# Self attention on one Trainium2 core: the maximum pass takes three operand pairs of two heads at a time, in two row groups of TensorE, and the two small transposes of a unit move into the middle of a key tile

## What is computed

```python
q = (src @ q_w).reshape(b, s, h, hd).transpose(0, 2, 1, 3)
k = (src @ k_w).reshape(b, s, h, hd).transpose(0, 2, 1, 3)
v = (src @ v_w).reshape(b, s, h, hd).transpose(0, 2, 1, 3)
scores = jnp.einsum('bhqd,bhkd->bhqk', q, k) / np.float32(np.sqrt(hd))
scale = jax.nn.sigmoid(jnp.einsum('bhsd,hd->bhs', q, scale_w)) * 2.0
scores = scores * scale[..., None]
aw = jax.nn.softmax(scores, axis=-1)
out = jnp.einsum('bhqk,bhkd->bhqd', aw, v).transpose(0, 2, 1, 3).reshape(b, s, d)
```

## Time and profile before

| | us |
|---|---|
| median of three runs (2272.37 to 2284.99) | 2282.37 |
| the profiled execution, whole | 2276.61 |
| its span in the trace | 2274.9 |
| self attention, first `first_scores` to the last transpose | 394.6 to 1225.4 |
| one unit in the steady part | 24.69 |

### The profile page before, as it was taken

The page is one execution under the profiler, slowest core; times in us unless marked ns, Lnnn a source line. Parts: engine busy times, 40 slices in busy tenths (PEclk is TensorE's granted clock), DMA queues, the critical chain, the costliest instruction groups (busy, mean ns, idle before and its releaser), DMA issues. The chain is left out here.

```text
span 2274.9 us, 32465 instructions
## 1 busy us (share of the span) xinstructions
PE 1776.4 (78%) x10156; PEld 854.8 (38%) x10157; DVE 1330.3 (58%) x2273; ACT 958.9 (42%) x1700; POOL 489.5 (22%) x518
## 2 busy tenths in 40 slices
PE   5899794899999999999996870799157996114997
PEld 3465452122222222222222650477134663002564
DVE  5344352888878788788870442566584544693221
ACT  3322273277767677677775320344233332001110
POOL 4200144300000000000000444333652001046343
PEclk8899897699999999999998885899669998556999
DMA  4000188111112211111103007121200004201352
GB/s 125 1 2 1 43 279 268 46 34 35 34 35 50 51 34 34 35 34 34 34 2 138 23 0 244 57 64 61 71 15 1 2 1 148 83 1 38 92 129 28
DMA packets 111976, 137.02 MB, mean 60 GB/s; under 512 B 14176, under 2 KB 88032, under 8 KB 111584
## 3 DMA queue, kind: packets, MB, share of 16 engines
q1 hardware_dynamic: 97008, 113.33, 16.9%
q0 software_dynamic: 9216, 16.79, 3.2%
q10 hardware_dynamic: 5616, 5.11, 0.7%
HBM read 78.31 MB, written 56.89 MB: 59 GB/s over the span
## 5 line engine op out<-in xcount | busy, mean ns | idle before, releaser
L962 DVE TENSOR_REDUCE sa_mfull<-sa_a 128x1 f32<-128x1024 f32 x512 | 609.5, 1221 | 158.3 <-PE sa_a L1058 157.8
L1035 ACT ACTIVATE sa_e<-sa_b 128x512 f32<-128x512 f32 x1024 | 539.4, 600 | 285.0 <-PE sa_b L1082 280.6
L1058 PE MATMUL sa_a<-sa_k,sa_q 96*128 96x512 bf16 x1024 | 322.5, 398 | 68.4 <-DVE sa_mfull L962 39.3
L1082 PE MATMUL sa_b<-sa_q,sa_k 98*128 98x512 bf16 x1024 | 317.8, 382 | 10.1 <-issue 6.9
L1092 PE MATMUL sa_ops<-sa_e,sa_v 128*17 128x512 f32 x2048 | 271.8, 603 | 0.7 <-ACT sa_e L1035 0.7
L1058 PEld LDWEIGHTS sa_a<-sa_k,sa_q 96*128 96x128 bf16 x1024 | 74.0, 98 | 367.8 <-issue 183.4
L1201 POOL TENSOR_TENSOR ao_var<-ao_mv,x_eps_pow 128x4 f32<-128x4 f32 x8 | 1.6, 201 | 871.0 <-DVE ao_mv L1300 871.0
L1082 PEld LDWEIGHTS sa_b<-sa_q,sa_k 98*128 98x128 bf16 x1024 | 99.5, 98 | 179.5 <-ACT sa_e L1035 77.6
L213 DVE TENSOR_REDUCE xa_mx<-xa_rows 128x16 f32<-128x1024 f32 x64 | 78.3, 1224 | 98.4 <-PE xa_rows L445 98.4
L360 ACT ACTIVATE xa_pT<-xa_cols 128x1024 f32<-128x1024 f32 x64 | 62.1, 1022 | 84.8 <-PE xa_cols L477 84.8
L2482 DVE TENSOR_TENSOR sw_hT<-sw_p,sw_act 128x512 f32<-128x512 f32 x32 | 22.1, 692 | 108.4 <-PE sw_p L2427 108.4
(11 more groups left out here) (322 smaller groups left out, 2747.0 us busy)
## 6 DMA issues: line engine op xcount, KB each, us to landing
sa_q<-q_parts SPq DMA_DIRECT2D x16, 768.0 KB, 6.0
sa_k<-k_parts SPq DMA_DIRECT2D x16, 768.0 KB, 8.7
tc_w<-in_L_ffn_W SPq DMA_DIRECT2D x24, 512.0 KB, 6.7
k_parts<-sp_kpart SPq DMA_DIRECT2D x16, 384.0 KB, 2.9
q_parts<-sp_qpart SPq DMA_DIRECT2D x16, 384.0 KB, 2.9
expert_in<-ao_zero SPq DMA_DIRECT2D x1, 4992.0 KB, 22.8
expert_out<-ex_xb ACTq DMA_DIRECT2D x39, 128.0 KB, 1.7
v_groups<-sp_vt SPq DMA_DIRECT2D x8, 544.0 KB, 3.6
```

Source lines behind the costliest of these rows:

```text
L962: nc.vector.tensor_reduce(mfull[par][:, k // CT, k % CT:k % CT + 1], aps[at][:].rearrange("p a b -> p (a b)"), axis=X, op=ALU.max).then_in ...
L1035: nc.scalar.activation(ex[kt % 2][:, head], bps[(2 * (2 * s + qc) + i) % 3][:], ACT.Exp, scale=SCALE).then_inc(exp_done, 1)
L1058: last = nc.tensor.matmul(aps[at][:, half], qs[s][0:KROWS, head, q0:q0 + P], ks[s][0:KROWS, head, half * CW:(half + 1) * CW], start=True, ...
L1082: nc.tensor.matmul(bps[(2 * (2 * s + qc) + i) % 3][:], ks[s][:, head, kt * P:(kt + 1) * P], qs[s][:, head, qc * CW:(qc + 1) * CW], start=T ...
```

## The change

- `PAIRS` is split into two subsets of three pairs (48 rows, `AROWS`): (0,1), (0,0), (1,0), and (0,2), (1,1), (2,0) of (k part, q part). DRAM holds the subsets apart. The maximum pass uses the first subset only; the scores use both.
- In SBUF the operand tiles have 112 rows (`BROWS`). Heads 0 and 1 of a group (`LOW`) have the first subset in rows 0 to 47, the second in 48 to 95, the maximum rows at 96, 97; heads 2 and 3 (`HIGH`) are mirrored, with the first subset in rows 64 to 111, the maximum rows at 0, 1 and the second subset at 2 to 49. Idle rows are set to zero once. The score matmuls read all 112 rows.
- `first_scores` makes one use out of two matmuls of 48 rows, one of head h on rows 0 to 47, one of head h+2 on rows 64 to 111, each 128 queries by 512 keys, into the two banks. DVE's maximum gives two values (one per head and key half) into `mhalf`. A new DVE instruction, `combine`, takes the larger of the halves of a whole unit (128 x 16) into `mfull`, and PE's transpose waits for that (`m_full`).
- `transpose_max` moves to behind `weigh_values` of key tile 2, ahead of the second `first_scores`, and `transpose_out` to the same place of key tile 4; DVE's `split_max` and `normalize` move with them. `transpose_max` now waits by `fill` like every other use.
- SP: k's store is twelve DMAs a chunk (six runs by two halves, none with a broadcast source), q's stays at six. A group's load is nine DMAs (four for the first subset, four for the second, v). The first three loads wait, between the subsets, for zeroed rows: set 0 for DVE (`idle_zeroed`), sets 1 and 2 for POOL (`zeroed`). The negated maxima come back in two DMAs instead of one.
- DVE zeroes four idle pieces (16 or 32 rows x 2048 bf16) of set 0 ahead of its first maximum; POOL zeroes eight for the sets 1 and 2 and then sets six pieces of ones (2 x 2048) where it had three (2 x 4096), each waited for.

```diff
-PAIRS = ((0, 0), (1, 0), (2, 0), (0, 1), (1, 1), (0, 2))
-KROWS = len(PAIRS) * DK
+PAIRS = (((0, 1), (0, 0), (1, 0)), ((0, 2), (1, 1), (2, 0)))
+KROWS = 6 * DK
+AROWS = KROWS // 2
...
-                q_runs = ((0, 3, 0, False), (3, 2, 0, False), (5, 1, 0, False))
-                k_runs = ((0, 3, 0, True), (3, 2, 1, True), (5, 1, 2, True))
+                q_runs = ((0, 0, 1, 0), (0, 1, 2, 0), (1, 0, 3, 0))
+                k_runs = ((0, 0, 1, 1), (0, 1, 1, 0), (0, 2, 1, 0), (1, 0, 1, 2), (1, 1, 1, 1), (1, 2, 1, 0))
...
+    PAIRED = GH // 2
+    BROWS = 64 + AROWS
+    LOW, HIGH = slice(0, PAIRED), slice(PAIRED, GH)
+    IDLE = ((slice(96, BROWS), LOW), (slice(32, 64), HIGH))
+    MAX_ROWS = ((slice(KROWS, KROWS + MROWS), LOW), (slice(0, MROWS), HIGH))
...
-                def load(g, s):
-                    sp.dma_start(qs[s][0:KROWS], q_parts[ds(g, 1)].rearrange("g h r t -> r (g h) t")).then_inc(q_loaded[s], 16)
-                    sp.dma_start(ks[s][0:KROWS], k_parts[ds(g, 1)].rearrange("g h r t -> r (g h) t")).then_inc(k_loaded[s], 16)
+                def load(g, s, first=False):
+                    for rows, heads in ((slice(0, AROWS), LOW), (slice(64, BROWS), HIGH)):
+                        for dst, parts in ((qs[s], q_parts), (ks[s], k_parts)):
+                            sp.dma_start(dst[rows, heads], parts[0, ds(g, 1), heads].rearrange("g h r t -> r (g h) t")
+                                         ).then_inc(a_loaded[s], 16)
+                    if first and s == 0:
+                        sp.wait_ge(idle_zeroed, 4)
+                    if first and s > 0:
+                        sp.wait_ge(zeroed, 4 * s)
...
                 def maximum(par, k, use, at):
+                    head, t, half = k // (2 * CT), k // 2 % CT, k % 2
                     dve.wait_ge(a_filled, use + 1)
-                    nc.vector.tensor_reduce(mfull[par][:, k // CT, k % CT:k % CT + 1], aps[at][:].rearrange("p a b -> p (a b)"),
-                                            axis=X, op=ALU.max).then_inc(a_used, 1)
+                    nc.vector.tensor_reduce(mhalf[par][:, half, head:head + PAIRED + 1:PAIRED, t], aps[at][:], axis=X,
+                                            op=ALU.max).then_inc(a_used, 1)
+
+                def combine(a, par, used):
+                    dve.wait_ge(a_used, used)
+                    nc.vector.tensor_tensor(mfull[:], mhalf[par][:, 0], mhalf[par][:, 1], ALU.max).then_inc(m_full, 1)
...
                         for kt in range(KT):
+                            if kt == 2 and not (isinstance(n, int) and n + 1 >= UNITS):
+                                combine(n + 1, (qc + 1) % 2, base + offset)
                             for which in range(2):
+                                if which == 1 and kt == 2 and not (isinstance(n, int) and n + 1 >= UNITS):
+                                    split_max(n + 1, base + offset, at(offset))
+                                    offset += 1
+                                if which == 1 and kt == 4:
+                                    normalize(n, base + offset, at(offset))
+                                    offset += 1
...
-                    for half in range(2):
-                        last = nc.tensor.matmul(aps[at][:, half], qs[s][0:KROWS, head, q0:q0 + P],
-                                                ks[s][0:KROWS, head, half * CW:(half + 1) * CW], start=True, stop=True)
+                    for rows, h in ((slice(0, AROWS), head), (slice(64, BROWS), head + PAIRED)):
+                        last = nc.tensor.matmul(aps[at][:, h // PAIRED], qs[s][rows, h, q0:q0 + P],
+                                                ks[s][rows, h, half * CW:(half + 1) * CW], start=True, stop=True)
...
+                                if head == 2 and kt == 2 and not (isinstance(n, int) and n + 1 >= UNITS):
+                                    transpose_max(n + 1, base + offset, at(offset))
+                                    offset += 1
+                                if head == 2 and kt == 4:
+                                    transpose_out(n, base + offset, at(offset))
+                                    offset += 1
                                 if head in (0, 2) and ahead(n, kt, head // 2):
```

More of the change, by code:

```diff
@@ L652, in store @@
                         for half in range(HALVES):
[L653 to L657, removed]
+                            for subset, pair, pairs, part in runs:
+                                rows = dram[subset, ds(4 * i + 2 * half, 2)].rearrange("g h (d r) t -> (g h d) r t", r=3)
+                                sp.dma_start(rows[:, pair:pair + pairs, par * CW:(par + 1) * CW],
+                                             parts[par][:, part:part + pairs, half]).then_inc(stored[par], 16)
                 batches(sp, store)
@@ L661, in _ @@
                     sp.wait_ge(v_stored[par], 16 * B)
-                    for stored in (q_stored, k_stored):
-                        sp.wait_ge(stored[par], 16 * B * RUNS)
+                    for stored, runs in ((q_stored, len(q_runs)), (k_stored, len(k_runs))):
+                        sp.wait_ge(stored[par], 16 * B * HALVES * runs)
             @block.vector
@@ L868, in max_use @@
             return first_use(a - 1) + 4
-        return first_use(a - 1) + 6
+        return first_use(a - 1) + 5
     def out_use(n):
@@ L873, in out_use @@
             return first_use(n) + (5 if n == UNITS - 2 else 0)
-        return first_use(n) + 9
+        return first_use(n) + 10
     with ExitStack() as ctx:
@@ L879, in self_attention @@
         sb, ps, sem = kit.sb, kit.ps, kit.sem
[L880 to L881 removed]
+        qs = [sb(f"q{i}", [BROWS, GH, S], bf16) for i in range(SETS)]
+        ks = [sb(f"k{i}", [BROWS, GH, S], bf16) for i in range(SETS)]
         vs = [sb(f"v{i}", [P, KT, GH, VW]) for i in range(SETS)]
         ex = [sb(f"e{i}", [P, GH, CW]) for i in range(2)]
[L884 removed]
+        mhalf = [sb(f"mhalf{i}", [P, 2, GH, CT]) for i in range(2)]
+        mfull = sb("mfull", [P, GH, CT])
         negm = sb("negm", [GH * CT, MROWS, P], bf16)
@@ L933, in body @@
                             sp.wait_ge(pv_done, 2 * KT * g)
-                        load(g + 2, (s + 2) % SETS)
+                        load(g + 2, (s + 2) % SETS, isinstance(g, int) and g == 0)
                     pass_max(2 * g + 1, s, 1)
@@ L946, in _ @@
             def _(pool):
+                for s in range(1, SETS):
+                    for i, (tile, (rows, heads)) in enumerate((tile, idle) for tile in (qs[s], ks[s]) for idle in IDLE):
+                        nc.gpsimd.memset(tile[rows, heads], 0.0).then_inc(zeroed, 1)
+                        pool.wait_ge(zeroed, 4 * (s - 1) + i + 1)
+                pool.wait_ge(idle_zeroed, 4)
                 for s in range(SETS):
-                    nc.gpsimd.memset(ks[s][KROWS:], 1.0).then_inc(ones_made, 1)
-                pool.wait_ge(ones_made, SETS + 2)
+                    for i, (rows, heads) in enumerate(MAX_ROWS):
+                        nc.gpsimd.memset(ks[s][rows, heads], 1.0).then_inc(ones_made, 1)
+                        pool.wait_ge(ones_made, 2 * s + i + 1)
                 pool.wait_ge(n2b_loaded, 16)
@@ L1001, in body @@
                                     offset += 1
[L1002 to L1010, removed]
+                nc.vector.memset(o_sb[:], 1.0).then_inc(out_cleared, 1)
+                nc.vector.memset(ops[:], 0.0).then_inc(out_cleared, 1)
+                for i, (tile, (rows, heads)) in enumerate((tile, idle) for tile in (qs[0], ks[0]) for idle in IDLE):
+                    nc.vector.memset(tile[rows, heads], 0.0).then_inc(idle_zeroed, 1)
                 for k in range(TILE_MAXIMA):
                     maximum(0, k, k, k % 2)
+                combine(0, 0, TILE_MAXIMA)
                 split_max(0, TILE_MAXIMA, 0)
@@ L1120, in body @@
                                     offset += 1
[L1121 to L1126, removed]
                 for k in range(TILE_MAXIMA):
                     first_scores(k, k, k % 2, 0, 0, 0)
-                transpose_max(0, TILE_MAXIMA, 0, TILE_MAXIMA)
+                transpose_max(0, TILE_MAXIMA, 0)
                 for k in range(EARLY):
```

52 lines of the change are left out of this document (31 added, 21 removed).

## The result

| | us |
|---|---|
| before, median of 4 runs | 2279.27 |
| changed, median of 4 runs (2213.72 to 2223.34) | 2220.91 |
| ratio, 95% interval | 0.974 (0.970 to 0.978) |
| span of the profiled execution, before and changed | 2274.9, 2221.6 |
| one unit, before and changed | 24.69, 22.73 |

The kernel became 58 us faster (2.6%). The prediction was 2210, within 2187 to 2246; its sum was -69 us.

What follows compares the result with a forecast made beforehand. PE was taken as the bound. Units -65.7, ends -1, start -3, `combine` +0.2 and SP +0.5 gave -69 us, the profiled 2276.6 becoming 2207.6 and the median 2213.4; it named 2210, range 2187 to 2246.

Steps and rivals of the forecast that it cites:

- A plain key tile: Self attention: two pairs save 0.436 us, three more switches cost 0.285; with ACT's limit a key tile takes 2.69 us.
- The step with ACT's limit: Plain key tile: fourth score matmul waits for ACT's first exponential, 1.08 us behind the first score, where PE's order gives 1.06.
- The transposes: Key tiles 2, 4 and 5: moved transposes cost 0.34 plus 0.66 us extra, 1.0 a unit instead of 2.13.
- The start: Attention's start: half the first load and DVE's zeroings save 3 us; `combine` and its waits add 0.2.
- the two ends of the stage: Unit 30 has only two key tiles with pairs, unit 0 runs partly at the lower clock: 1 us more saved.
- its own sign: Prediction is wrong if a plain key tile is outside 2.6 to 2.75 us or a non-attention stretch changes over 2 us.
- The projections: SP's twelve k stores take at most 7.8 us and fit the 12.9 us chunk; last q store later, 0.5 us taken.
- That the pairs are worth nothing: Rival: switches at 0.17 us each, or a showing weight load, eat the pairs' gain; 2243 us, chance 0.10.
- That the two matmuls run one behind the other: Rival: a pair of 48-row matmuls costs 0.44 us, a key tile 3.10; 2301 us, chance 0.06.
- more: Rival: switches beside a 48-row pair cost near nothing, a key tile takes about 2.5 us; 2165 us, chance 0.08.
- SP's queue did not become the bound: Rival: in the projections SP's issues take 16.7 us a chunk, 3.8 more than 12.9; 2240 us, chance 0.08.
- The clock stayed at 0.99: Rival: granted clock falls as matmuls fill 0.81 of a key tile, not 0.93; half the 240 gives 2462, chance 0.05.

Runs made afterwards that it cites:

- one switch less in the variant: Changed kernel with both pairs of a key tile put behind head 0's score matmul, the transposes staying behind `weigh_values`: 2203.09 us, ratio to before 0.968.

## Why the prediction was right

**A plain key tile.** Forecast 2.69, measured 2.71, before 2.82. Pair 0.22, switches of 0.1 also for the layouts of 48 rows, five of them. The Trainium skill ("TensorEngine Tiling (Array Packing)", "Tiling Modes") says that a change of the mode drains the array; this trace agrees, with 0.10 us for each, and one switch less in the variant gave 0.11 back. The step with ACT's limit was not needed: PE's own order already made the 1.08 us, and halving ACT's work changed 0.02 us a unit. By PE's order alone the prediction had 2.67, 0.04 too little, and ACT's step added 0.02 of it for a reason that did not hold: that half of the error was made good by luck, 0.16 us a unit or 5 us in the whole.

**The transposes.** Forecast 1.0 us extra a unit, measured 0.36 + 0.71 = 1.07; before 2.13. Most of the 0.07 is the four transposes, taken at the 0.44 us of the earlier trace rows where behind `weigh_values` they hold 0.49. `combine` took 0.18 and not 0.14, beside PE. The waits were where they were put: 0.16 in front of the pair behind `transpose_max` (what half the maximum took away; forecast 0.13), 0.12 in key tile 5 for `normalize` (forecast 0.13).

**The unit** is 22.73 and not 22.5: the mis-sized terms are eight times 0.02 and once 0.07, 0.23 x 30 = 7 us of the 11 that the prediction missed. Starts were read to 0.01 us, and the switch was taken at 0.095 where the rows gave 0.09 to 0.10; eight key tiles with three new switches each make of that 0.1 us a unit.

**The turns of the loop** were not in the sum at all: 3.8 us in the first traces (14.5 less 10.7), 3.4 in the second, some 2.5 of it time at the lower clock.

**The start** gave 5.5 us, forecast 2.8: the zeroings were cheaper than their bound (0.91 against 1.9 us), so DVE was free before the loads had landed, and the half load set the start (3.7 us). The other 1.8 us, in the 28 maxima, had no term in the sum. That PE's side-by-side matmuls bring them is likely (with both in one row group the stretch took 36.3 us), but no run isolates it.

Sum inside the attention, first instruction to last transpose: 841.0 to 779.9, -61.1 us, where the prediction had -69.5: 7 and 3.8 less, 2.7 more, and 0.3 less at the two ends of the stage (forecast 1, measured 0.7). The two traces as a whole differ by only 53.3 us, because stages that the change does not touch took 1.7 us more ahead of the first k store and 5.6 more behind the attention, and the projections' end 0.4. By its own sign (over 2 us outside the attention) the prediction would be wrong; the sign was set too tight, for untouched stages differ by up to 10 us from trace to trace.

**The projections** were forecast 0.5 us slower through SP's queue, and their end is 0.4 later. But it is not SP's issues: twelve took 5.8 us and not 7.8, q's burst started as far behind k's start as before (6.73 us in both), and the last issue ends 0.3 us sooner behind the last k burst. What follows the issues takes longer; the later landing of smaller pieces would fit, but was not tried.

**The rivals.** That the pairs are worth nothing, fell with the variant that has them alone. That the two matmuls run one behind the other, fell with their starts, 2 to 4 ns apart. That a switch beside a 48-row pair costs near nothing (*more*), fell with its 0.10 us. SP's queue did not become the bound (k's and q's 18 issues fill 9.2 us of a chunk of 12.9). The clock stayed at 0.99 although matmuls fill less of the time; in unit 0 it was 0.58 and 0.59 over the first nine microseconds in the two traces of the changed kernel, 0.50 and 0.85 in those of the kernel before, so no difference is shown there.

## What to carry to other kernels

Two matmuls of up to 64 rows in different row groups run in the time of one, but each change of layout around them costs about 0.1 us, nearly half of what a 512-column pair saves; put such pairs next to each other (0.11 us a key tile here). Both pairs behind `weigh_values`, where there is a switch anyway, would need one switch less still; that was not tried. Where two buffers are taken in turn, a small transpose in the sequence makes the next big fill wait for a reduction that has just begun; put the transpose before the fill that would wait anyway, behind the longest matmul group. Changing the order of uses was worth as much here as the change of the matmul.

## What was not expected of the hardware

A turn of the hardware loop costs PE 3.3 to 4.0 us of branch, of which 2 to 3 show, and at most turns then a stretch at the lower clock: 3.6 to 4.9 us a turn on the mean, 11 to 15 us in the whole stage. That is what the change saves in five to eight units.

Inside the loop key tile 4 takes 3.42 us, in the units written out behind it 3.31; with the moves alone it is 3.53 and 3.42. What the 0.11 us are was not tried.
